# Local attention loop: queries and keys turned two units ahead of use, first output projection over units 11 to 13, and another order at the loop's end

## The reference

```python
h = shift_token(x)                       # half of the features moved down by one token
q, k, v = split(h @ wqkv)                # 8 heads of 64
q = l2norm(q) * qs;  k = l2norm(k) * ksc
q, k = rotary_xpos(q, k)
o = local_attention(q, k, v)             # softmax over a window of 64 and the one before it
x = x + o @ wo
h = layer_norm(shift_token(x))
a, g = split(h @ w1 + b1)
x = x + (a * gelu(g)) @ w2 + b2
```

## Time and profile before

| | us |
|---|---|
| median of 3 runs (lowest to highest) | 790.16 (789.87 to 793.35) |
| the profiled execution | 788.48 |
| its span, first to last instruction | 786.7 |
| busy: PE / DVE / ACT / POOL | 626.8 / 542.5 / 499.9 / 239.5 |
| mean granted TensorE clock | 0.81 of full |

### The profile page before, as it was taken

One profiled execution on the slowest core, in us unless ns is written; L12 is line 12 of the kernel. 1 busy time (PEld: TensorE's weight loads), 2 busy tenths in 40 slices (PEclk: granted clock), 3 DMA queues, 4 the chain that ended last, 5 costly groups with the idle time before them and its releaser, 6 DMA issues.

```text
span 786.7 us, 13264 instructions
## 1 busy us (share of the span) xinstructions
PE 626.8 (80%) x4802; PEld 377.4 (48%) x4802; DVE 542.5 (69%) x1119; ACT 499.9 (64%) x1187; POOL 239.5 (30%) x237
## 2 busy tenths in 40 slices
PE   7679986767789988966889798695878779578776
PEld 3312222354356655644555455543656544356654
DVE  7783328747899889767787877569754457984444
ACT  4459997661778878715477666385576439667642
POOL 5030006011789978970200000000554100055400
PEclk9779999998555555595599999896599999678999
DMA  8400000000000000000000000000000000000000
GB/s 277 157 1 1 1 1 1 0 1 0 1 2 1 1 2 2 1 1 0 1 1 2 1 1 2 1 1 0 2 2 2 1 0 0 1 2 2 1 1 27
DMA packets 9204, 9.88 MB, mean 13 GB/s; under 512 B 2890, under 2 KB 7988, under 8 KB 9012
## 3 DMA queue, kind: packets, MB, share of 16 engines
q1 hardware_dynamic: 9140, 9.04, 3.5%
HBM read 8.51 MB, written 0.52 MB: 11 GB/s over the span
## 4 chain that ended last, share of the span: by engine, by line
PE 43%; DVE 30%; ACT 15%; issue 9%; POOL 2%; DMA 1%; ACTq 0%; DVEq 0%; POOLq 0%
PE ps L1691 4%; PE ps L1431 4%; PE ps L1594 4%; DVE s_nmB L1086 4%; PE ps L1674 3%; ACT arena L571 3%; PE ps L1581 3%; PE ps L1711 3%; PE ps L1502 2%; ACT dev L698 2%; PE ps L1474 2%; PE ps L1893 2%; PE ps L1781 2%; ACT arena L674 2%; DVE s_nmD L1351 2%
## 5 line engine op out<-in xcount | busy, mean ns | idle before, releaser
L415 POOL TENSOR_SCALAR arena<-arena,s_rB,s_zpu 128x512 uint8<-128x512 f32 x128 | 115.9, 943 | 35.2 <-DVE s_rB L1059 34.7
L609 ACT ACTIVATE arena<-ps,s_nmB 128x512 f32<-128x512 f32 x128 | 86.6, 683 | 31.7 <-DVE s_nmB L1086 31.2
L631 ACT ACTIVATE arena<-ps,s_nmx 128x512 f32<-128x512 f32 (+3 forms) x128 | 60.7, 527 | 50.2 <-DVE s_nmx L1184 49.7
L1086 DVE TENSOR_REDUCE s_nmB<-ps 128x2 f32<-128x1024 f32 x64 | 77.3, 1216 | 6.9 <-PE ps L1581 6.6
L449 POOL COPY arena<-arena 64x512 f32<-64x512 f32 x16 | 13.0, 814 | 220.9 <-PE ps L1774 219.0
L1179 DVE TENSOR_REDUCE s_nmx<-ps 128x1 f32<-128x512 f32 (+3 forms) x128 | 56.6, 483 | 21.5 <-PE ps L1677 21.0
L571 ACT ACTIVATE arena<-ps 128x1024 f32<-128x1024 f32 x64 | 60.9, 1026 | 6.5 <-PE ps L1486 6.5
L1594 PE MATMUL ps<-cst,arena 128*128 128x128 f32 x256 | 61.0, 416 | 1.7 <-POOL arena L415 0.8
L1437 PE MATMUL ps<-ones 128*128 128x512 f16 x134 | 40.9, 457 | 24.2 <-ACT s_rn L562 3.6
L1581 PE MATMUL ps<-staged 8*128 8x512 f16 x128 | 46.7, 585 | 11.7 <-ACT arena L609 10.9
L1594 PEld LDWEIGHTS ps<-cst,arena 128*128 128x128 f32 x256 | 48.7, 218 | 14.6 <-POOL arena L415 8.0
(11 more groups left out here) (337 smaller groups left out, 1510.4 us busy)
## 6 DMA issues: line engine op xcount, KB each, us to landing
w_d<-in_wqkv SPq DMA_DIRECT2D x2, 768.0 KB
vec<-in_vec SPq DMA_DIRECT2D x1, 1200.0 KB, 10.8
vec<-in_vec SPq DMA_DIRECT2D x1, 960.0 KB, 8.0
w_h<-in_w SPq DMA_DIRECT2D x2, 341.0 KB
x_tok<-in_x SPq DMA_DIRECT2D x1, 512.0 KB, 4.0
arena<-in_w_f SPq DMA_DIRECT2D x2, 256.0 KB, 7.7
rope<-in_rope SPq DMA_DIRECT2D x1, 512.0 KB, 9.2
w_do<-in_wo SPq DMA_DIRECT2D x2, 256.0 KB
```

Source lines behind the costliest of these rows:

```text
L415: nc.gpsimd.tensor_scalar(u8[:, n % 4, j // 2, :, 2 * (j % 2)], prob[:, n % 2, j * 512:j * 512 + 512], sm("rB", 8)[:, c:c + 1], sm("zpu", ...
L609: nc.scalar.activation(prob[:, n % 2, j * 512:j * 512 + 512], ps[:, j, :], ACT.Exp, bias=sm("nmB", 8)[:, c:c + 1], accum_out=sm("sumB", 8) ...
L631: nc.scalar.activation(probC[:, n % 2, at(qt):at(qt) + w], ps[:, bank, col:col + w], ACT.Exp, bias=nmx[:, TB * b + qt, h:h + 1]).then_inc( ...
L1086: free(V.tensor_reduce(sm("nmB", 8)[:, c:c + 2], ps[:, 2 * half:2 * half + 2, :], X, ALU.max, negate=True), "maxB")
```

## The change

Four edits, in both layers:

1. **Pieces one unit earlier.** Five pieces are turned ahead of the loop in place of four, and unit u turns piece number u+5 in place of u+4. PE's wait for the copy of the piece turned in unit u-1, where u is a multiple of 4, is gone. Ahead of unit 0, DVE runs two rotation steps in place of one, and the factors of the second batch (`factors(1)`) come behind one more step of unit 0.
2. **First projection spread.** Tiles 0 and 1 are projected at unit 11, tile 2 at unit 12, tile 3 at unit 13 (before: 0 and 1 at 12, 2 and 3 at 13). There is no piece to turn any more in these units. DVE adds in three portions.
3. **Second projection grouped.** Tiles 4 and 5 are projected together at turn 17, tiles 6 and 7 at turn 18, behind `turn_e(0)`, which moves ahead of them.
4. **The table of the square root** is loaded on ACT ahead of its last copy of the loop, by an activation on one column (`load_table`), not by `roots_d`.

```diff
+        FIRST_PIECES = ((0, 2), (0, 3), (0, 0), (0, 1), (1, 0))
+        PROJECTED_AT = {11: (0, 1), 12: (2,), 13: (3,)}
+        def projected_o(t):
+            return ps[:, (6, 7, 0, 6)[t], 256:256 + P]
...
@@ ScalarE
-                            for k, i in enumerate((2, 3, 0, 1)):
-                                turned_qk(0, i, 1 - k % 2)
+                            for k, (p, i) in enumerate(FIRST_PIECES):
+                                turned_qk(p, i, 1 - k % 2)
...
-                    if u < UNITS - 4:
-                        turned_qk(u // 4 + 1, u % 4, u % 2)
+                    if u + 5 < UNITS:
+                        turned_qk((u + 5) // PIECES, (u + 5) % PIECES, u % 2)
...
+                    if u == UNITS:
+                        load_table(ACT.Sqrt)
...
@@ VectorE
                 next(rest)
+                next(rest)
...
+                        if u == 11:
+                            add_o(0, 2, ps[:, 6:8, 256:256 + P])
                         if u in (12, 13):
-                            add_o(2 * (u - 12), 2, ps[:, 6 * (u % 2), 256:512])
+                            add_o(u - 10, 1, projected_o(u - 10).unsqueeze(1))
...
-                        if u == 0:
-                            factors(1)
...
                     next(rest, None)
+                    if u == 0:
+                        factors(1)
...
@@ TensorE
-                            pe.wait_ge(sem["qk_ev"], UNITS * l + min(u + 3, UNITS))
-                        if u % 4 == 0:
-                            pe.wait_ge(sem["qk_ev"], UNITS * l + u + 4)
-                        if u < UNITS - 4:
-                            turn_piece(u // 4 + 1, u % 4, u % 2)
-                        if u in (12, 13):
-                            for k in range(2):
-                                project_o(2 * (u - 12) + k, ps[:, 6 * (u % 2), 256 + P * k:256 + P * k + P])
-                        if u >= 14:
-                            pe.wait_ge(sem["do_ev"], 3 * l + u - 13)
+                        pe.wait_ge(sem["qk_ev"], UNITS * l + min(u + 4, UNITS))
+                        if u + 5 < UNITS:
+                            turn_piece((u + 5) // PIECES, (u + 5) % PIECES, u % 2)
+                        for t in PROJECTED_AT.get(u, ()):
+                            project_o(t, projected_o(t))
+                        if u >= 13:
+                            pe.wait_ge(sem["do_ev"], 4 * l + u - 12)
...
-                    if u >= UNITS:
-                        if u == UNITS:
-                            pe.wait_ge(sem["expD"], 4 * (U - 1))
-                            pe.wait_ge(sem["lnsq"], B * l + 1)
-                        t = TB + u - UNITS
-                        project_o(t, ps[:, 0, P * (t - TB):P * (t - TB) + P])
-                project_o(T - 1, ps[:, 0, 3 * P:4 * P])
...
+                    if u > UNITS:
+                        if u == UNITS + 1:
+                            pe.wait_ge(sem["expD"], 4 * (U - 2))
+                        else:
+                            turn_e(0)
+                        for t in range(2 * u - 2 * UNITS + 2, 2 * u - 2 * UNITS + 4):
+                            project_o(t, ps[:, 0, P * (t - TB):P * (t - TB) + P])
...
-                turn_e(0)
                 hidden(0, 0)
```

More of the change, by code:

```diff
@@ L110, in build @@
         rope = sb("rope", [P, 4, TB, DHD])
-        primed = sb("primed", [P, 12])
+        primed = sb("primed", [P, 16])
         condT = sb("condT", [P, B])
@@ L1306, in add_o @@
                     dve.wait_ge(sem["do_mm"], T * l + t + n)
-                    add(f[:, t:t + n, :], f[:, t:t + n, :], o.rearrange("p (t c) -> p t c", t=n), "do_ev")
+                    add(f[:, t:t + n, :], f[:, t:t + n, :], o, "do_ev")
                 def less_mean(b):
@@ L1396, in _ @@
                 put_o(l, T - 1)
-                add_o(TB, TB, ps[:, 0, :])
+                add_o(TB, TB, ps[:, 0, :].rearrange("p (t c) -> p t c", t=TB))
                 send(1)
@@ L1813, in s_d, with turn_e @@
                     ins.then_inc(sem["sD"], 1)
+                def turn_e(b):
+                    pe.wait_ge(sem["lnD"], B * l + b + 1)
+                    transposes(f"e{l}", lambda t: devL[:, t, :], tiles=range(TB * b, TB * b + TB))
                 def pv_d(t, v):
@@ L1833, in _ @@
                         pe.wait_ge(sem["qk_ev"], UNITS * l + k - 1)
-                    turn_piece(0, i, 1 - k % 2)
+                    turn_piece(p, i, 1 - k % 2)
                 pe.wait_ge(sem["d_ev"], T * (l + 1))
@@ L1869, in _ @@
                         pv_d(t, u - 3)
-                    if u >= UNITS:
-                        if u == UNITS:
-                            pe.wait_ge(sem["expD"], 4 * (U - 1))
-                            pe.wait_ge(sem["lnsq"], B * l + 1)
-                        t = TB + u - UNITS
-                        project_o(t, ps[:, 0, P * (t - TB):P * (t - TB) + P])
-                project_o(T - 1, ps[:, 0, 3 * P:4 * P])
-                def turn_e(b):
-                    pe.wait_ge(sem["lnD"], B * l + b + 1)
-                    transposes(f"e{l}", lambda t: devL[:, t, :], tiles=range(TB * b, TB * b + TB))
+                    if u > UNITS:
[5 more added lines that the diff above has]
+                            project_o(t, ps[:, 0, P * (t - TB):P * (t - TB) + P])
                 def hidden(b, c):
@@ L1888, in hidden @@
                     if c == 1:
-                        pe.wait_ge(sem["do_ev"], 3 * (l + 1))
+                        pe.wait_ge(sem["do_ev"], 4 * (l + 1))
                     if q >= 2:
```

## The result

| | before | after |
|---|---|---|
| first comparison, median (lowest to highest), 4 runs each | 790.01 us (788.75 to 793.35) | 780.16 us (777.16 to 780.92) |
| ratio, 95% interval | | 0.9862 (0.9822 to 0.9902) |
| profiled execution / its span | 788.48 / 786.7 us | 780.48 / 778.7 us |
| busy: PE / DVE / ACT / POOL | 626.8 / 542.5 / 499.9 / 239.5 us | 623.2 / 544.8 / 501.6 / 235.8 us |
| mean granted TensorE clock | 0.81 | 0.81 |

The change made the kernel 1.4% faster, 780 us where 774 was forecast and 766 to 784 was the range. Two later comparisons gave 0.9757 (0.9725 to 0.9788) and 0.9782 (0.974 to 0.9824). In those the changed kernel took 777.04 and 779.18 us, hardly other than here, and the kernel before 795.77 and 797.91 us in place of 790.

What follows compares the result with a forecast made beforehand. It took half-clock PE, then the circle over POOL, then nearly full PE and ACT as bounds, plus single PE stops for ACT's copies. Gains 6.9 + 4.8 + 4.4 = 16.1 from 788.48 gave 772.4, 774 as measured; range 766 to 784.

Steps and rivals of the forecast that it cites:

- unit 0 later: Loop start: one more DVE rotation step ahead of unit 0 makes it start 1.4 us late.
- unit 1 later: Scores of unit 1 stand behind a piece waiting for a rotation ended in unit 0; unit 1 is 1.8 us late.
- part 1: Pieces one unit earlier, units 0 to 8: the wait of unit 8 goes; gain 2.8 and 4.1 us, sum 6.9.
- part 2: First projection at units 11 to 13: PE's wait of 1.69 and a piece of 0.66 go; 2.4 us per layer.
- Parts 3 and 4: Loop's end, second projection grouped and early table load: PE becomes the late one; gain 2.2 us per layer, 4.4 in all.
- The late start of 0.7 at unit 5: What stays at unit 5 of the later loop start: between 0 and 1.8 us, taken as 0.7.
- 7.35: Units 5 to 7: time for two units, in us, kept from the profile before and used in both layers.
- The step from unit 7 to 8: Put at 3.0 us, like units 8 to 11, as unit 7 has one rotation step left.
- The sign that I gave: Reduce of unit 8 comes 35 us behind a first reduce itself 1.4 later; before 37.3 us.
- My own test: Part 1 is wrong if waits for POOL ahead of the transposes grow as much as waits for the copies shrink.
- The first rival: The circle over POOL takes all of part 1, which then gives 0: 781 us; chance 0.16.
- the circle over POOL: From reduce over reciprocal, POOL's multiply of 1.93 us, transposes and value products to the scores two units on.

Runs made afterwards that it cites:

- experiments 1 and 2: Kernel before with the `primed` buffer four columns wider, 795.63 us; the same plus second projection grouped, `turn_e` moved ahead and early table load, 792.53 us.
- experiment 4: Changed kernel with PE's wait for the copy of the previous unit's piece put back at units 4, 8 and 12; 792.04 us, ratio 0.9909.
- experiment 3: Changed kernel with tiles 0 and 1 projected at unit 12, 2 and 3 at unit 13 again; 781.60 us, ratio 0.9814.
- experiment 1: Kernel before with only the `primed` buffer four columns wider; 795.63 us, ratio 1.0001.

## Why the prediction was right

The forecast of 774 us missed the first comparison by 6 us: the change gained 9.9 us there in the medians, where 16.1 was forecast. By its own steps, from the profiles of before and after, measured from the same point ahead of each loop:

| step | forecast, both layers | measured |
|---|---|---|
| unit 0 later | 1.4 per layer | 1.46 / 1.45 |
| unit 1 later | 1.8 per layer | 1.8 |
| part 1, gain at unit 8 | 2.8 + 4.1 = 6.9 | 2.98 + 4.05 = 7.0 |
| given back between units 8 and 10 | 0 | -1.06 - 0.55 = -1.6 |
| part 2, units 10 to 13 | 4.8 | 2.51 + 2.74 = 5.25 |
| parts 3 and 4, unit 13 to `hidden` | 4.4 | 2.32 + 2.78 = 5.1 |
| sum | 16.1 | 15.8 |

**Part 1 was right in size, in part by luck.** Unit 8 came where I put it in this pair of profiles, by terms that cancel. The late start of 0.7 at unit 5 was 0.6 in layer 0 and -0.3 in layer 1. For units 5 to 7 I took 7.35 in both layers, though layer 1 had taken 8.99 before, and gave no reason; it took 7.90 / 8.71. The step from unit 7 to 8, which I put at 3.0, took 2.39 / 2.67. It is this one step, with the stop in it, that made most of the gain: before it took 6.54 / 6.12. And over the three profiles of the old loop code (before, experiments 1 and 2) unit 8 stands at 38.1 on average, over those of the changed kernel at 35.0: 3.1 per layer, 6.2 us in both. One term was missing: the transposes ahead of unit 9 wait for POOL as well (1.56 at 586.48), because DVE is only just through with its rotations, and 1.6 us go back by unit 10. One reading was incomplete: at unit 4 I saw no stop, but in layer 1 PE waited there 1.20 for ACT's copy.

What I had wrong is what the stop is worth. I priced it by DVE's idle time; experiment 4 shows that in the new order the waits alone are worth 6.1 / 5.6 at unit 8 against the first profile of the changed kernel (7.15 / 6.55 against the second), and that the new order with the waits kept has unit 8 at 41.58 / 40.67, where the kernel before has 38.43 / 39.15. So moving the pieces costs 3.2 / 1.5 and dropping the waits gives 6.1 / 5.6; I had both too small, the cost at 0.7 and the worth at 3.5 / 4.8, and their difference right. Why the kept wait at unit 8 grew from 2.07 to 3.02 no run tells. The sign that I gave, unit 8 at 35 us behind the first reduce, doesn't follow from my own sum either: 579.3 less 546.3 is 33.0, and 32.82 / 32.48 was measured.

**My own test misfired.** I wrote that part 1 is wrong if the waits for POOL grow by as much as those for the copies shrink. Over both layers the waits for copies ahead of pieces sank by 5.1 us and those for POOL ahead of the transposes grew by 5.0, for the whole kernel by group and releaser:

```profile
L1786 PE MATMUL ps<-cst,arena 128*128 128x128 f32 x128 | 25.8, 349 | 17.7 <-DVE arena L1292 11.3 <-ACT arena L675 6.1 <-DVE arena L324 0.2
...
L1873 PE MATMUL ps<-cst,dev 128*128 128x128 f32 x64 | 12.1, 319 | 7.6 <-POOL dev L467 7.5
L1873 PE MATMUL ps<-cst,sq 128*128 128x128 f32 x64 | 11.9, 315 | 10.2 <-POOL sq L467 10.1
```

(before, the groups of L1774 and L1859 had 11.2 for the copies, and 2.6 and 10.0 for POOL.) And the time still fell. By another count the test would not have fired: the stop ahead of the projections of unit 12 (1.69 / 1.70) went with part 1 as well, and with it (3.4 in the group of L1781 before, none after) the waits for copies sank by 8.5. A test whose outcome hangs on such a count is a poor one, and it looked at the wrong engine. From 575 to 585 us, units 5 to 8, DVE is busy for 4.86 of every 5 us in the changed kernel (windows in experiment 4), so it sets the pace there, and a wait of PE costs nothing; before, DVE stood idle ahead of the reduces of units 7 and 8. Waits of PE for ACT were on the path, those for POOL are mostly beside it.

The first rival (POOL takes part 1) gave 781, near what the first comparison measured, but for another reason: its mechanism would have left unit 8 where it was. POOL's multiplies beside rotations take 1.40 to 1.93 in the changed kernel, before 1.33 to 1.93, so they are not stretched further. The step from unit 5 to 7 grew from 7.35 to 7.90 in layer 0, but DVE has no idle time ahead of these reduces: its own rotations set that step, not the circle over POOL. The Trainium skill ("GPSIMD Engine Reference", Specifications) says that DVE instructions with two SBUF inputs contend with GpSimd for its way to SBUF. The trace agrees: 1.04 at 585.39 and after, when the rotations are over, and 1.40 to 1.93 beside them.

**Part 2 was right in sum and wrong in its parts.** The 1.69 I booked for it goes with part 1 already (experiment 3), and so does the piece of unit 11, which the new order no longer turns there; what part 2 itself shows in the loop is 0.95 per layer, which I hadn't booked. The combined step of 5.25 us holds both.

**Parts 3 and 4 were right**, 3.2 to 4.1 us alone and 5.1 in the profiles, and PE was the late one, as I had it; part 4 contributes nothing that can be told.

**Where the 6 us are.** In the loops and what follows them, up to `hidden`, 15.8 of the 16.1 us arrived in this pair of profiles. In the profile of after they are offset by 6.0 us ahead of the first loop (its end at 549.72, before 543.72), 0.25 between the layers and 1.5 at the kernel's end. None of these is in changed code, and they move from one execution to the next: the point ahead of the first loop was at 547.66 and 546.31 in experiments 1 and 2, which have the old code there, and at 549.72, 546.53 and 547.70 in three profiles of the changed kernel. Over all thirteen profiles it lies between 543.7 and 552.6, and it goes with the granted clock from 340 to 400 us, which was 0.69 in the profile of before and 0.61 in that of after. So 543.72 was the early end of what this code gives, and the loops of that profile had no lower clock behind the stop of unit 12. In the later comparisons the kernel before took 796 to 798 us and the change gained 17 to 19 us, a little more than forecast. In experiment 1 `hidden` stands at 82.93 / 81.81, in the second profile of the changed kernel at 72.12 / 72.21: 20.4 us, where the pair of the first comparison gives 15.8. That the steps come so near to the forecast is thus partly luck: the forecast and this table use the same profile of before. Why the kernel before was 6 to 8 us faster in the first comparison I did not settle: four runs each were made there, and chip and execution can't be told apart by these.

## What to carry to other kernels

A wait of the engine that does the matmuls has two prices, its own length and the clock behind it; here stops of 9.7 us, put back, cost 11.4 to 12.0. Turning something earlier needs its producers earlier as well: the extra rotation step looked like a cost and carried the whole gain of part 1. One profile of the kernel before is a poor yardstick for differences of 1%. And before a growing wait counts as a loss, look at which engine is full in that stretch.

## What the runs showed of the hardware that I had not expected

- The same stop of 1.7 us ahead of the same two projections was followed by work at either clock: 2.02 us in one execution, 3.61 in another.
- Code that is the same reached the end of its last norm reduction ahead of the first loop between 543.7 and 552.6 us, over all thirteen profiles. The granted clock from 340 to 400 us was 0.66 to 0.69 in those that ended by 547.9, and 0.60 or 0.61 in those from 549.7 on. That is up to 1.1% of the kernel's time, more than some of the effects under test.
- Five matmuls of some 0.25 us each, put where PE paused, kept the clock at 1.00 through the 15 us that followed, and brought `hidden` 1.1 to 2.0 us nearer to unit 15. Fourteen ahead of a pause of 3.2 us raised it to 1.00 while they ran; behind the pause it was at 0.50, as without them.
- A table load on ACT took 1.28 us and delayed nothing as long as it lay in an idle time; the next instruction began right behind it (614.66 + 1.28 = 615.94, the next at 615.95).
